# One plan for three engines in causal attention: other costs, longer rings, paired value products

## What is computed

```python
x = L0_attn_x                                     # 1 x 4096 x 256, fp32
h = layernorm(x) * (1 + ca) + sa                  # sa, ca, ga, sb, cb, gb from silu(c) @ wmod
q, k, v = h @ Wq.T, h @ Wk.T, h @ Wv.T            # 16 heads of 16; q and k turned by their position
scores = einsum('bhqd,bhkd->bhqk', q, k) * 16 ** -0.5 + mask   # causal, 4096 x 4096 a head
attn = softmax(scores)                            # fp32
x = x + ga * ((attn @ v) @ Wo.T)
h = layernorm(x) * (1 + cb) + sb
x = x + gb * ffn(h)                               # 8 experts, 256 -> 1024 -> 256, gelu
```

## Time and profile before

| | |
|---|---|
| median of 3 runs | 2092.42 us (2088.43 to 2095.24) |
| profiled execution | 2090.41 us |
| its span | 2088.6 us |
| attention, from the first unit to the last value product | 147.5 to 1735 us |
| PE, DVE, ACT busy over the span | 91%, 81%, 65% |

### The profile page before, as it was taken

The page is one execution under the profiler, slowest core; times in us unless marked ns, Lnnn a source line. Parts: engine busy times, 40 slices in busy tenths (PEclk is TensorE's granted clock), DMA queues, the critical chain, the costliest instruction groups (busy, mean ns, idle before and its releaser), DMA issues. The chain is left out here.

```text
span 2088.6 us, 36838 instructions
## 1 busy us (share of the span) xinstructions
PE 1894.6 (91%) x13224; PEld 888.2 (43%) x13224; DVE 1701.6 (81%) x2969; ACT 1348.3 (65%) x2675; POOL 236.6 (11%) x185
## 2 busy tenths in 40 slices
PE   7843899999999999999999999999999996869998
PEld 4521333333434433343433333344333324538887
DVE  5962899998959999996899999769999803978886
ACT  3411466677687777768777776787777793226553
POOL 4720000000000000000000000000000002544442
PEclk9965799999999999999999999999999998989999
DMA  5865000000003000000300000010000003203331
GB/s 179 226 165 112 10 9 9 9 8 2 10 2 86 10 9 9 10 10 2 85 10 9 10 9 9 3 55 9 2 2 2 1 2 137 70 11 109 106 112 34
DMA packets 58667, 86.90 MB, mean 42 GB/s; under 512 B 9412, under 2 KB 31428, under 8 KB 58504
## 3 DMA queue, kind: packets, MB, share of 16 engines
q1 hardware_dynamic: 58504, 84.70, 14.6%
HBM read 58.06 MB, written 20.97 MB: 38 GB/s over the span
## 5 line engine op out<-in xcount | busy, mean ns | idle before, releaser
L940 DVE TENSOR_REDUCE mx<-banks 128x1 f32<-128x512 f32 (+3 forms) x2304 | 1305.1, 638 | 202.3 <-PE banks L841 189.4
L908 ACT ACTIVATE prob<-banks 128x512 f32<-128x512 f32 (+3 forms) x2304 | 1116.8, 619 | 373.7 <-PE banks L817 267.1
L817 PE MATMUL banks<-q_aug,k_aug 52*128 52x512 f32 (+3 forms) x2304 | 532.7, 461 | 59.5 <-issue 26.1
L879 PE MATMUL banks<-prob,v_all 128*17 128x512 f32 (+3 forms) x4608 | 580.1, 576 | 0.0
L841 PE MATMUL banks<-k_aug,q_aug 48*128 48x512 f32 (+3 forms) x2304 | 518.7, 450 | 56.7 <-DMA later_h<-in_later 26.1
L817 PEld LDWEIGHTS banks<-q_aug,k_aug 52*128 52x128 f32 x2304 | 227.7, 188 | 493.1 <-ACT prob L908 306.6
L841 PEld LDWEIGHTS banks<-k_aug,q_aug 48*128 48x128 f32 x2304 | 233.5, 190 | 306.8 <-ACT prob L908 193.1
L979 POOL CAST nm_p<-nm 128x16 fp32r<-128x16 f32 x32 | 6.8, 214 | 1510.0 <-DVE nm L946 1510.0
L879 PEld LDWEIGHTS banks<-prob,v_all 128*17 128x17 f32 x4608 | 77.0, 96 | 164.9 <-issue 86.9
L849 PE MATMUL banks<-id_h,later_h 64*128 64x128 bf16 x1024 | 77.5, 228 | 0.0
L825 PE MATMUL banks<-later_h,id_h 64*128 64x128 bf16 x1024 | 76.0, 225 | 0.0
(11 more groups left out here) (113 smaller groups left out, 1471.6 us busy)
## 6 DMA issues: line engine op xcount, KB each, us to landing
parts_scratch<-p SPq DMA_DIRECT2D x64, 256.0 KB, 4.1
w_s<-in_w SPq DMA_DIRECT2D x16, 1024.0 KB, 5.5
xs<-in_x SPq DMA_DIRECT2D x16, 512.0 KB, 4.6
k_aug<-parts_scratch SPq DMA_DIRECT2D x64, 128.0 KB, 3.2
q_aug<-parts_scratch SPq DMA_DIRECT2D x64, 128.0 KB, 2.6
cs<-in_rope SPq DMA_DIRECT2D x8, 512.0 KB, 5.8
k_aug<-parts_scratch SPq DMA_DIRECT2D x64, 64.0 KB, 3.1
q_aug<-parts_scratch SPq DMA_DIRECT2D x64, 64.0 KB, 2.6
```

The source lines that it names most:

```text
L817: mm = nc.tensor.matmul(bank(banks[r])[:, q0:CW], keys[rows], q_aug[rows, n % QRING, b, q0:CW], start=True, stop=True)
L879: mm = nc.tensor.matmul(pv[32 * j:32 * j + VW, q0:CW], v_all[:, g, kb, j, :], prob[:, s % PROBS, j, q0:CW], start=(kb == 0), stop=(s == LA ...
L908: nc.scalar.activation(prob[:, s % PROBS, j, q0:CW], bank(from_bank)[:, q0:CW], ACT.Exp, scale=float(HD) ** -0.5).then_inc(act_read, 1)
L940: nc.vector.tensor_reduce(mx[:, n % QRING, r, b, t, kc:kc + 1], bank(from_bank)[:, 0:unit_width(i)], AX_X, ALU.max).then_inc(dve_read, 1)
```

## The change

- The planner's costs: PE's modelled time is now a drain when the kind of work changes (DRAIN) and a weight load (WEIGHTS) where it shows; the times from PE to ACT and DVE go from 312 and 232 ns to 212 and 212, a masked pair from 125 to 214 ns more, a turn from 530 to 436; PACE and the biases have other values.
- Value products: a product starts only when the exponentials of two steps have been planned (at a task's last step one is enough), and once one has been issued the next has a bonus of 3000, so that two follow each other.
- Units: take_pair() prefers two neighbouring banks. Where it gets them, VectorE takes both heads' maxima by one tensor_reduce of 128 x 2 x 512; elsewhere, as before, by two. One semaphore step is counted for either.
- Masks: id_h and later_h are fp32r. They are loaded as fp32 into o_sb, POOL copies them (masks_cut), and TensorE's first unit waits for that.
- Rings: KRING 12 to 14, QRING 5 to 6, LEAD 3 to 4.

```diff
-KRING = 12
-QRING = 5
+KRING = 14
+QRING = 6
 PROBS = 4
-LEAD = 3
+LEAD = 4
...
-    def begin_at(ready, to_wide):
-        if wide == to_wide and ready > pe - RELOAD:
-            return max(pe + RELOAD, ready)
-        return max(pe + (TO_VALUES if to_wide else FROM_VALUES if wide else 0), ready)
+    def take_pair():
+        banks, ready = take(2)
+        for b in BANKS:
+            if b + 1 in free and max(free[b], free[b + 1]) <= max(ready, pe - WEIGHTS["pair"]):
+                return [b, b + 1], max(free[b], free[b + 1])
+        return banks, ready
+
+    def begin_at(ready, to):
+        if mode == to == "pair":
+            return max(pe, ready + WEIGHTS["pair"])
+        return max(pe + (0 if mode == to else DRAIN[mode]), ready) + (0 if mode == to else WEIGHTS[to])
...
-        if val < pair // JP and not (norm and LAST[STEPS[val][0]] == val):
-            begins = begin_at(max(exp_end[val], pv_free if STEPS[val][1] == 0 else 0.0), True)
-            choices.append((VALUES_BIAS - VALUES_STEP * (pair // JP - val) + (VALUES_AGAIN if wide else 0)
+        if val + (0 if mode == "values" or STEPS[val][1] == TILES * (TASKS[STEPS[val][0]][1] + 1) - 1 else 1) < pair // JP and not (norm and LAST[STEPS[val][0]] == val):
+            begins = begin_at(max(exp_end[val], pv_free if STEPS[val][1] == 0 else 0.0), "values")
+            choices.append((VALUES_BIAS - VALUES_STEP * (pair // JP - val) + (-3000 if mode == "values" else 0)
...
-            for r in range(RTILES):
-                on_dve(("most", at, r, banks[r]), begins + w * PE_COLUMN + masks + PE_TO_DVE,
-                       w * DVE_COLUMN + DVE_FIXED, banks[r])
+            ready = begins + w * PE_COLUMN + masks + PE_TO_DVE
+            if banks[1] == banks[0] + 1:
+                on_dve(("most", at, None, banks), ready, RTILES * w * DVE_COLUMN + DVE_FIXED, *banks)
+            else:
+                for r in range(RTILES):
+                    on_dve(("most", at, r, banks[r:r + 1]), ready, w * DVE_COLUMN + DVE_FIXED, banks[r])
...
-PV_COLUMN = 853 / 512
-TO_VALUES, FROM_VALUES, RELOAD = 214, 114, 95
-MASK_NS, TURN_NS = 125, 530
+PV_COLUMN = 1.667
+WEIGHTS = {"pair": 107, "values": 15, "turn": 15}
+DRAIN = {"pair": 85, "values": 115, "turn": 93}
+MASK_NS, TURN_NS = 214, 436
...
-PE_TO_ACT, PE_TO_DVE, ACT_TO_PE, DVE_TO_PE = 312, 232, 164, 140
+PE_TO_ACT, PE_TO_DVE, ACT_TO_PE, DVE_TO_PE = 212, 212, 168, 135
...
-PACE = 4.28
-MOST_BIAS, SMALL_BIAS = -471, 627
-VALUES_BIAS, VALUES_STEP, VALUES_AGAIN = 1100, 34, 1073
+PACE = 6.96
+MOST_BIAS, SMALL_BIAS = -191.76, -368.68
+VALUES_BIAS, VALUES_STEP, VALUES_AGAIN = 2091.85, 34.29, 1716.87
...
-    id_h = sb("id_h", [P, RTILES, P], BF16)
-    later_h = sb("later_h", [P, RTILES, P], BF16)
+    id_h = sb("id_h", [P, RTILES, P], F32R)
+    later_h = sb("later_h", [P, RTILES, P], F32R)
...
-            def most(i, r, from_bank):
+            def most(i, r, banks):
                 n, t, kc, b = UNITS[i]
-                dve.wait_ge(most_done, RTILES * i + r + 1)
-                nc.vector.tensor_reduce(mx[:, n % QRING, r, b, t, kc:kc + 1], bank(from_bank)[:, 0:unit_width(i)], AX_X,
-                                        ALU.max).then_inc(dve_read, 1)
+                heads = slice(r, r + 1) if len(banks) == 1 else slice(0, RTILES)
+                dve.wait_ge(most_done, RTILES * i + heads.stop)
+                nc.vector.tensor_reduce(mx[:, n % QRING, heads, b, t, kc],
+                                        bank(banks[0], len(banks)).rearrange("p (r s) -> p r s", s=CW)[:, :, 0:unit_width(i)],
+                                        AX_X, ALU.max).then_inc(dve_read, 1)
...
+            pool.wait_ge(masks_in, 32)
+            nc.gpsimd.tensor_copy(id_h[:, :, :].rearrange("p h c -> p (h c)"), o_sb[:, 0, 0:RTILES * P])\
+                .then_inc(masks_cut, 1)
+            nc.gpsimd.tensor_copy(later_h[:, :, :].rearrange("p h c -> p (h c)"), o_sb[:, 1, 0:RTILES * P])\
+                .then_inc(masks_cut, 1)
```

More of the change, by code:

```diff
@@ L102, in plan @@
     pe = act = dve = 0.0
-    wide = False
+    mode = "pair"
     free = {b: 0.0 for b in BANKS}
@@ L131, in on_act, with on_dve @@
             free[bank], reader[bank] = act + ACT_TO_PE, ("act", len(act_order))
-    def on_dve(item, ready, ns, bank):
+    def on_dve(item, ready, ns, *banks):
         nonlocal dve
@@ L136, in on_dve @@
         dve_order.append(item)
-        if bank in free:
-            free[bank], reader[bank] = dve + DVE_TO_PE, ("dve", len([0 for d in dve_order if d[0] != "nm"]))
+        for b in banks:
+            free[b], reader[b] = dve + DVE_TO_PE, ("dve", len([0 for d in dve_order if d[0] != "nm"]))
     def maxima_of(n):
         nonlocal turn
-        on_dve(("nm", n), 0.0, NM_NS, None)
+        on_dve(("nm", n), 0.0, NM_NS)
         turn = (dve + CUT_NS, n)
@@ L151, in plan @@
                 banks, ready = take(2)
-                begins = begin_at(max(ready, rows[main]), False)
+                begins = begin_at(max(ready, rows[main]), "pair")
                 choices.append((act - begins + PACE * max(begins - pe, 0), "score", begins, banks))
@@ L156, in plan @@
             if n <= main + LEAD and not (turn and late_nm is not None) and (n < QRING or n - QRING in main_end):
-                banks, ready = take(2)
-                begins = begin_at(max(ready, main_end[n - QRING] + LOAD_NS if n >= QRING else 0.0), False)
+                banks, ready = take_pair()
+                begins = begin_at(max(ready, main_end[n - QRING] + LOAD_NS if n >= QRING else 0.0), "pair")
                 choices.append((dve - begins + MOST_BIAS + PACE * max(begins - pe, 0), "most", begins, banks))
@@ L162, in plan @@
                 banks, ready = take(1)
-                begins = begin_at(max(ready, small[0]), False)
+                begins = begin_at(max(ready, small[0]), "turn")
                 choices.append((SMALL_BIAS + PACE * max(begins - pe, 0), kind, begins, banks))
-        if val < pair // JP and not (norm and LAST[STEPS[val][0]] == val):
-            begins = begin_at(max(exp_end[val], pv_free if STEPS[val][1] == 0 else 0.0), True)
-            choices.append((VALUES_BIAS - VALUES_STEP * (pair // JP - val) + (VALUES_AGAIN if wide else 0)
+        if val + (0 if mode == "values" or STEPS[val][1] == TILES * (TASKS[STEPS[val][0]][1] + 1) - 1 else 1) < pair // JP and not (norm and LAST[STEPS[val][0]] == val):
+            begins = begin_at(max(exp_end[val], pv_free if STEPS[val][1] == 0 else 0.0), "values")
+            choices.append((VALUES_BIAS - VALUES_STEP * (pair // JP - val) + (-3000 if mode == "values" else 0)
                             + PACE * max(begins - pe, 0), "values", begins, None))
@@ L188, in plan @@
                         sp_order.append((act, "keys", k))
-            pair, pe, wide = pair + 1, begins + max(w * PE_COLUMN + PE_FIXED, PE_LEAST) + masks, False
+            pair, pe, mode = pair + 1, begins + max(w * PE_COLUMN + PE_FIXED, PE_LEAST) + masks, "pair"
         elif kind == "most":
@@ L204, in plan @@
                     late_nm = n
-            at, pe, wide = at + 1, begins + max(w * PE_COLUMN + PE_FIXED, PE_LEAST) + masks, False
+            at, pe, mode = at + 1, begins + max(w * PE_COLUMN + PE_FIXED, PE_LEAST) + masks, "pair"
         elif kind == "turn":
             pe_order.append(("turn", turn[1], None, banks, after))
-            pe, wide = begins + TURN_NS, False
+            pe, mode = begins + TURN_NS, "turn"
             on_act(("turn", turn[1], None, banks[0]), pe + PE_TO_ACT, CW * ACT_COLUMN + ACT_FIXED, banks[0])
@@ L220, in plan @@
             pe_order.append(("values", val, None, None, None))
-            pe, wide = begins + step_width(val) * PV_COLUMN, True
+            pe, mode = begins + step_width(val) * PV_COLUMN, "values"
             pv_end[val] = pe
@@ L245 @@
 DVE_READS = [item for item in DVE_ORDER if item[0] != "nm"]
-DVE_AT = {item[:3]: i + 1 for i, item in enumerate(DVE_READS)}
+MOST_AT = {item[1]: i + 1 for i, item in enumerate(DVE_READS) if item[0] == "most"}
 def build(nc, x, wqk, wvT, woT, lnsb, attnT, attnb, w1, b1, w2, b2, nextT, nextb, cvec, wmod,
@@ L729, in attend_block @@
     act_read, dve_read = sem("act_read"), sem("dve_read")
+    masks_cut = sem("masks_cut")
     nm_done, cut_done, linv_done = sem("nm_done"), sem("cut_done"), sem("linv_done")
@@ L769, in _ @@
             load_queries(0)
-            sp.dma_start(id_h[:, :, :], a["halves"]).then_inc(masks_in, 16)
-            sp.dma_start(later_h[:, :, :], a["later"]).then_inc(masks_in, 16)
+            sp.dma_start(o_sb[:, 0, 0:RTILES * P], a["halves"].rearrange("p h c -> p (h c)")).then_inc(masks_in, 16)
+            sp.dma_start(o_sb[:, 1, 0:RTILES * P], a["later"].rearrange("p h c -> p (h c)")).then_inc(masks_in, 16)
             sp.dma_start(m_rows[0:MCOLS, :, :], a["ownrows"]).then_inc(ones_in, 16)
@@ L882, in values @@
                 mm.then_inc(pv_done, 1)
-            pe.wait_ge(masks_in, 32)
+            pe.wait_ge(masks_cut, 2)
```

(8 more changed lines are left out.)

4 lines of the change are left out of this document (2 added, 2 removed).

## The result

The changed kernel took 2236.13 us (median of 4 runs, 2224.08 to 2243.17), beside 2091.5 for the kernel before: a ratio of 1.0688 (95% interval 1.066 to 1.0715), slower by about 145 us. I had forecast 2058 and a range of 1960 to 2135.

The account below looks back on a forecast made before the run. VectorE's maxima, fed through seven banks, were taken as the bound beside units, ScalarE's exponentials without them. Terms -75 - 63 + 93 + 3 + 8 = -34 took 2090.4 to 2056, median 2058 us; range 1960 to 2135.

Parts of the forecast that it names:

- VectorE's line: Attention's time as start, all VectorE's maxima with pauses, then task 31's scores; every term was summed on this chain.
- the doubles' term: Two value products together on PE: VectorE pauses 0.7 us in about 240 doubles, 168 us less 75, net +93 us.
- LEAD 4: Next quad's chunk 3 runs in VectorE's three pauses: 75 of 79 us less, bounds 40 and 79.
- rival 4: In VectorE's pauses LEAD gives back 40 us alone, since PE's work is only moved: 2093 us; chance 0.07.
- One reduce for two banks: VectorE's joined maxima save 0.065 us fixed cost each: 63 us less at 85% joined, bounds none and 75.
- rival 1: Double value products empty both queues: VectorE pauses 1.1 us (sign: over 0.84), term +189, 2154 us; chance 0.2.
- 75 us of short waits: VectorE's 177 short waits, 74.7 us behind value products and scores, taken as replaced by the pauses behind doubled products.
- The price of a change of mode: Joining value products spares PE 0.3 us each, 88 us in all; no gain for VectorE while PE waits for banks.
- Masks: fp32r weight loads in 512 masked pairs: 26 us of PE, of which VectorE feels 3 us; bounds -10 and +20.
- Rings: More DMAs on SP's queue ahead of the first scores: 8.3 us later, counted +8; bounds 0 and +12.
- Last task: Task 31's scores, set by ScalarE and untouched by the doubled value products: 0, bounds -2 to +5.
- Other costs: The planner's other costs move single orders: counted at 0, bounds -20 to +20.

Follow-up runs that it names:

- e7: Kernel before with every row maximum taken over 7/8 of its columns only (part of the computation left out): 2052.55 us, ratio 0.9829.
- e3: Kernel before with LEAD = 4 alone, both rings as before: 2097.93 us, ratio 1.0008.
- e14: Kernel before with LEAD 2 instead of 3: 2236.97 us, ratio 1.0684.
- e12: Kernel before with the first spread issued early, LEAD 4, RELOAD 60 and planner biases favouring scores over units: 2030.34 us, ratio 0.9708.
- e15: e12 with LEAD 3 instead of 4, same biases, beside the kernel before: 2099.7 us, ratio 1.0037.
- e13: Changed kernel with both doubled value products and joined maxima undone, the rest kept: 2089.49 us, ratio 0.9989 to the kernel before.
- e1: Changed kernel with doubled value products undone (one step's exponentials suffice, no bonus for a second): 2103.07 us, ratio 1.0048 to the kernel before.
- e4: Kernel before with joined maxima alone (929 of 1152 units joined), LEAD 3: 2144.56 us, ratio 1.0243.
- e5: Kernel before with the fp32r masks alone; plan, rings and LEAD as before: 2106.02 us, ratio 1.0067.
- e9: Kernel before with KRING 14 and QRING 6 alone: 2101.88 us, ratio 1.0036.
- e11: Kernel before with the first spread of maxima issued ahead of the loads that fill the rings: 2072.12 us, ratio 0.9916.
- e2: Kernel before with doubled value products alone (272 stand together instead of 3), costs and biases as before: 2406.57 us, ratio 1.1497.
- e10: Kernel before with six banks instead of seven for units and score pairs, planned anew: 2257.5 us, ratio 1.0797.

## Why the prediction was wrong

The step that failed is the base of the sum: "I make the sum on VectorE's line". In it each microsecond of VectorE counted in full. The runs show 37 of 130 (e7). VectorE's maxima and the chain of scores were about level in the kernel before, and each step that gave to one took from the other; in the changed kernel the scores are the later of the two, by the lag of 14.5 us at task 31. The second step is the size of the doubles' term. In numbers: my sum was -75 - 63 + 93 + 3 + 8 = -34. The runs give 133 for the doubles, 14 for the joins, 14 for the masks, 9 for the rings, and some -25 for LEAD with the new costs, together 145. That it comes out even is no proof, since the last term is the remainder.

- *LEAD 4*, 75 us less: nothing by itself (e3). My rival 4 named the mechanism, PE's work only moved, at 40 us; it took all. From 2 to 3 LEAD is worth 145 us (e14); from 3 to 4 it is worth something only with biases that give the freed time to the scores (e12, e15: 69 us).
- *One reduce for two banks*, 63 us less: 14 us more (e13 against e1) or 52 more (e4). The fixed part is saved as worked out: four joined reduces take 4.62 us, with one lasting 1.22, so one starts every 1.13 us. The price, two banks held longer, I had named and put into the next term at nothing of its own. Only 521 units were joined, 45% for my 85%.
- *Doubles*, 93 us more: 133 (e1) with the joins in place. The mechanism was the one described, and it is rival 1: a pause of 0.96 us in the mean against my 0.7, its 1.1, and over the 0.84 at which I had put its sign. I had counted 240 doubles, there are 214, so the number hid a part of the miss. What I left out is that ScalarE stops as well (1.69 us), and that the refill is slow; and I took off 75 us of short waits that did not go away.
- The price of a change of mode, PE's 0.3 us a double, is worth nothing here as a gain: it was spared where both readers then ran dry. The Trainium skill (TensorEngine Tiling (Array Packing), Key Properties) says that a change of tiling mode drains TensorE; the rows agree in sign.
- *Masks*, 3 us more: 14 to 16 (e5). The 26 us of PE were right in size (its busy time in e5 rose by 26.3); that VectorE's line would hide them was wrong. The Trainium skill (TensorE: Matmul & The Clock Gate, Weight-path perf modes) says that the fast weight load is for types other than FP32. The loads of 97 ns in bf16 and 198 ns in fp32r agree.
- *Rings*, 8 us more: 9 (e9). *Last task*, 0: 0. *Other costs*, 0: with doubles and joins undone the changed kernel is at 2089, though masks and rings cost 14 and 9; so, if the parts add, the new costs and biases with LEAD 4 gave some 25 us back. Which of the two did was not run.

The rows had the warning: PE's weight loads waited 193 us for banks of ScalarE while VectorE had 74.6 of 78 us. Two nearly full readers and a full PE meant a shared bound, and I took the fullest reader for it.

There was a second warning, in the kernel itself: plan() also returns PLANNED, the time at which its own modelled engines end. It needs no chip. Modelled and measured, each against the kernel before (e12 against e11, as the model has no start of attention):

| | PLANNED, us | modelled | measured |
|---|---|---|---|
| kernel before | 1482 | | |
| changed kernel | 1582 | +100 | +145 |
| doubles (e2) | 1718 | +236 | +314 |
| joined maxima (e4) | 1522 | +40 | +52 |
| LEAD 2 (e14) | 1535 | +53 | +145 |
| LEAD 4 (e3) | 1476 | -6 | +2 (-3 to +6) |
| six banks (e10) | 1595 | +114 | +165 |
| other biases, LEAD 4 (e12) | 1437 | -45 | -42 |

The changed kernel's row has its own cost constants; the others have those of the kernel before (e12 with RELOAD 60). The model is too mild with every loss, but it has the sign of each large change, the doubles and the joins among them.

## What to carry to other kernels

Where several engines live on one small pool of buffers, don't sum on the fullest engine: price a change by how long it holds buffers and by which of the parallel chains arrives last, and try the engine's speed first by giving it an eighth less to do. Where a planner models the engines, read its own total before and after. A long uninterrupted block on the engine that fills the buffers must be shorter than what the buffers hold for all its readers together. More room ahead helps only with a policy that gives the freed time to the later chain.

## What was not expected of the hardware

The granted clock fell in the kernels that stall more: over the span 0.949 before, 0.925 in the changed kernel, 0.902 in e2, 0.912 in e14, and 0.958 in e12. Windows of attention, before and changed:

```profile
205.00:1735.00 1530.00, 1474.22 (x11370) 575.89 (x11368) 1303.80 (x2355) 1139.73 (x2352) 13.94 (x62) 0.97 0.06 14
...
205.00:1885.00 1680.00, 1511.50 (x11452) 679.73 (x11452) 1295.84 (x1862) 1156.24 (x2366) 13.90 (x62) 0.94 0.05 12
```

With levels of 1.2 and 2.4 GHz, 0.94 of 1680 us is about 200 us at the lower one, and 0.97 of 1530 us about 90. In this stretch of the changed kernel PE never stood over 2.5 us at a time; all its idle time there is 168 us, and 56 before. What made the clock fall is not shown by a run. What it costs can be estimated from the 50 runs of the kernel before that stand beside the experiments, at 0.942 to 0.952: a clock lower by 0.01 goes with about 14.5 us more. By that slope the lower clock would be some 30 of the changed kernel's 145 us, and some 70 of e2's 314, which is an estimate far outside the 50 runs.

A joined reduce over two PSUM banks cost no more than its columns and one fixed part: 1.13 us from one to the next, 2 x 0.533 + 0.065 by the earlier trace rows.
